# Routing the tiles of the first image between the products of the second image's dynamic convolution

## What is computed

```
x = x + relu(group_norm(conv1x1(concat[xn, dyn_1(xn), dyn_4(xn), dyn_8(xn), dyn_12(xn)])))   # xn = layer norm of x over channels
t = tokens(x)                                        # 2 x 9216 tokens of 256 values
l = layer_norm(t)                                    # over the 256 values
logits = l @ router.T                                # 8 experts
two best experts per token, their softmax weights divided by their sum
t = t + l + sum over the two of weight_e * (gelu(l @ w1[e] + b1[e]) @ w2[e] + b2[e])
```

## Time and profile before

| | us |
|---|---|
| median of three runs | 2617.31 |
| the profiled execution | 2616.45 |
| its span, first to last instruction | 2614.6 |

### The profile page before, as it was taken

How to read it: one execution, slowest core, us unless ns; L and a number is a source line. 1 busy time by engine, 2 the same in 40 slices (tenths; PEclk the granted TensorE clock), 3 DMA queues, 4 the chain that set the end, 5 groups by cost and what they waited for, 6 DMA issues and landing times.

```text
span 2614.6 us, 61081 instructions
## 1 busy us (share of the span) xinstructions
PE 2046.2 (78%) x20292; PEld 1918.8 (73%) x20293; DVE 1624.7 (62%) x4238; ACT 1187.8 (45%) x2441; POOL 1026.5 (39%) x1390
## 2 busy tenths in 40 slices
PE   5887699999688867999994766750799999995332
PEld 4777499999678757999993766650799999994222
DVE  3554475666555545656665867663577899885644
ACT  4654233333256533333333544440577777773211
POOL 4444012233234411223320677777455566563000
PEclk9999599999899977999996655555899999997555
DMA  4332156677433214656766897753566555555887
GB/s 122 91 88 68 47 174 157 158 179 176 123 85 85 79 43 132 170 142 170 174 160 186 277 325 264 257 189 131 164 195 206 172 162 159 150 158 177 289 296 271
DMA packets 328031, 434.91 MB, mean 166 GB/s; under 512 B 86586, under 2 KB 253114, under 8 KB 326778
## 3 DMA queue, kind: packets, MB, share of 16 engines
q1 hardware_dynamic: 273618, 315.07, 42.9%
q0 software_dynamic: 41024, 97.10, 10.7%
q10 hardware_dynamic: 13200, 20.19, 2.1%
HBM read 278.46 MB, written 159.94 MB: 168 GB/s over the span
## 4 chain that ended last, share of the span: by engine, by line
PE 46%; DMA 17%; POOL 15%; issue 10%; DVE 5%; ACT 4%; DVEq 2%; SPq 1%; POOLq 0%; ACTq 0%
PE ps_y L381 16%; POOL expert_in L1786 8%; DMA expert_out<-e_out,dest 7%; PE ps L381 6%; POOL taps L1752 6%; PE ps_o L854 6%; PE ps_a L381 5%; PE ps_b L790 5%; DMA o_y<-expert_out 3%; DMA o_acc<-res_scratch 2%; ACT g_rows L1059 2%; PE ps_f L762 2%; DMA expert_in<-c_ln,pos 2%; PE ps_o L841 1%; PE ps_x L967 1%
## 5 line engine op out<-in xcount | busy, mean ns | idle before, releaser
L381 PE MATMUL ps_y<-cat_hi,wp 128*128 128x288 f32 x2048 | 469.5, 305 | 1.8 <-DVE cat_lo L1370 1.8
L1774 POOL DMA_DIRECT2D patches<-rows_scratch x352 | 194.8, 598 | 651.5 <-PE ps_o L854 492.4
L1809 POOL DMA_INDIRECT expert_out<-e_out,dest x304 | 310.3, 1021 | 237.4 <-DMA expert_out<-e_out,dest 117.4
L1786 POOL DMA_INDIRECT expert_in<-c_ln,pos x288 | 294.4, 1022 | 186.8 <-DVE pos L1515 92.1
L381 PEld LDWEIGHTS ps_y<-cat_hi,wp 128*128 128x128 f32 x2048 | 343.2, 189 | 2.0 <-DVE cat_lo L1370 2.0
L1137 ACT ACTIVATE cat_hi<-ps_o 128x288 fp32r<-128x288 f32 (+1 forms) x576 | 200.1, 386 | 252.9 <-PE ps_o L854 164.2
L381 PE MATMUL ps_y<-cat_lo,wp 128*128 128x288 f32 x1024 | 301.4, 294 | 0.0
L1370 DVE SCALAR_TENSOR_TENSOR cat_lo<-ps_o,cat_hi 128x288 fp32r<-128x288 f32 (+1 forms) x576 | 219.4, 419 | 129.8 <-ACT cat_hi L1137 129.6
L1752 POOL TENSOR_TENSOR taps<-taps,g_rows 96x108 f32<-96x108 f32 (+1 forms) x432 | 200.7, 494 | 242.2 <-ACT g_rows L1059 238.5
L381 PE MATMUL ps<-e_hi,w_now 128*128 128x256 f32 x1216 | 243.8, 284 | 1.2 <-issue 1.1
L381 PE MATMUL ps<-w,h_hi 128*128 x1216 | 234.5, 291 | 5.6 <-DVE h_lo L1658 5.6
(11 more groups left out here) (181 smaller groups left out, 4774.1 us busy)
## 6 DMA issues: line engine op xcount, KB each, us to landing
e_x<-expert_in SPq DMA_DIRECT2D x152, 260.0 KB
o_y<-expert_out SPq DMA_DIRECT2D x48, 768.0 KB, 5.3
patches<-rows_scratch SPq DMA_DIRECT2D x160, 192.0 KB
patches<-rows_scratch SPq DMA_DIRECT2D x256, 108.0 KB
patches<-rows_scratch SPq DMA_DIRECT2D x192, 112.0 KB
x_in<-in_x SPq DMA_DIRECT2D x48, 384.0 KB, 3.3
rows_scratch<-rows_st SPq DMA_DIRECT2D x48, 384.0 KB, 3.1
y_scratch<-y_acc SPq DMA_DIRECT2D x16, 1152.0 KB, 11.6
```

What stands on the lines that cost most here:

```text
L381: mm = eng.matmul(out, lhs[p], rhs[q], start=start and n == 0, stop=stop and n == 2)
L1774: pool.dma_start(patch_target(s, n), patch_source(m, s, n)).then_inc(patch_pooled[s % RING], 16)
L1786: pool.indirect_dma_start(out=xs_dram, out_offset=bass.IndirectOffsetOnAxis(ap=at, axis=0), in_=c_ln[:, v, k // TT, k % TT], in_offset=Non ...
L1809: pool.indirect_dma_start(out=ys_dram, out_offset=bass.IndirectOffsetOnAxis(ap=at, axis=0), in_=e_out[:, u, j], in_offset=None).then_inc(e ...
```

## The change

The first image is routed during the product stage of the second image. A `slot` is a place between two branch products of that stage, one in each step but the first, and two in a step of kind 3, which makes 79. In 72 of them PE turns one tile of 128 tokens and multiplies it by the router (`turn_tile`), ACT and DVE do the statistics, the norm and the residual of that tile, and once for six tiles DVE does `choose` and `place` in pieces of one to four instructions that stand between its other work. The logits are taken from the raw token and corrected by `router_sum` (the sum of the router's rows), so that the second transpose falls away for these tiles. SP loads the blocks and stores a residual per tile, POOL adds x and the convolution's output (`add_block`, one TENSOR_TENSOR of 768 values a partition) and issues the 144 scatters, three in a step. All of this has psum in one bank, `ps_k`, taken from `ps_b`, so `band` now fills one bank in two halves, the second after the step's second tick, in the product stages of both images. The ring of patches falls from 4 to 3. The group norm of the first image is computed at the start of the second image's first stage, six constants are loaded at the program's start, and the routing stage has only the 12 pairs of the second image. EARLY (residual groups kept in SBUF for the combination) falls from 30 to 28 of 48. `w1`, `b1`, `b2` and eight fills are now issued behind the first two pairs' loads of the routing stage; before they were issued halfway through it.

```diff
-RING = 4
+RING = 3
-EARLY = 30
+EARLY = 28
-            ps_b = psum(r1, "ps_b", [128, 2, 512])
+            ps_b = psum(r1, "ps_b", [128, 512])
+            ps_k = psum(r1, "ps_k", [128, 512])
...
+                def turn_tile(t):
+                    j, k = divmod(t, TT)
+                    pe.wait_ge(r_x1, j + 1)
+                    for c in range(CC):
+                        pe.transpose(ps_k[:, c * 128:(c + 1) * 128], r_x[:, j % 2, c, k * 128:(k + 1) * 128], ident[:])
+                    for c in range(CC):
+                        mm = pe.matmul(ps_k[:, 256 + t % TP * E:256 + (t % TP + 1) * E], r_x[:, j % 2, c, k * 128:(k + 1) * 128],
+                                       router[:, c], start=c == 0, stop=c == CC - 1)
+                    mm.then_inc(r_tok, 1)
...
-                        band(s + 1)
+                        band(s + 1, 0)
                     for n in range(CC * parts(s)):
                         branch(s, n // parts(s), n % parts(s))
+                        k = slot_at(m, s, n)
+                        if k is not None:
+                            slot(k)
                         if s and n in (1, 3):
                             project(s - 1, n // 2, 0)
                             project(s - 1, n // 2, 1)
+                        if n == 1 and s + 1 < STEPS:
+                            band(s + 1, 1)
...
+                        t = slot_at(m, s, n, 1)                      # ACT
+                        if t is not None and t < ITILES:
+                            norm_tile(t)
+                            if t % TT == 1 and (t + 2) // TT < ITILES // TT:
+                                relu_block((t + 2) // TT)
...
+                def add_block(j):                                    # POOL
+                    pool.wait_ge(r_relu, j + 1)
+                    flat = lambda z: z.rearrange("p c k -> p (c k)")
+                    pool.tensor_tensor(flat(r_x[:, j % 2]), flat(r_x[:, j % 2]), flat(r_y[:, j % 2]), ALU.add).then_inc(r_x1, 1)
+                def scatter_rows(p, q):
+                    if q == 0:
+                        pool.wait_ge(r_placed, p + 1)
+                    for k in range(3 * q, 3 * q + 3):
...
                 for s in range(STEPS):
+                    while m and blocks < ITILES // TT and slot_step(3 * blocks - 2) + 2 <= s:
+                        add_block(blocks)
+                        blocks += 1
+                    while m and quarters < 4 * CPAIRS and placed_step(quarters // 4) + 3 + quarters % 4 <= s:
+                        scatter_rows(quarters // 4, quarters % 4)
+                        quarters += 1
                     shared = [n for n in range(loads(s)) if second_queue(s, n)]
                     if shared and s >= RING:
                         pool.wait_ge(out_ready, m * UNITS + unit(s - RING + 1))
```

More of the change, by code:

```diff
@@ L443, in build, with slot_at, slot_step, pair_at @@
         UNITS = unit(STEPS)
+        slot_ticks = []
+        for s_ in range(1, STEPS):
+            first = 2 if kind(s_) == 1 and s_ > UNITS1 else 1
+            slot_ticks += [unit(s_) + first] + ([unit(s_) + 5] if kind(s_) == 3 else [])
+        slot_of_tick = {u: k for k, u in enumerate(slot_ticks)}
+        step_of_tick = [s_ for s_ in range(STEPS) for n_ in range(CC * parts(s_))]
+        def slot_at(m, s, n, later=0):
+            k = slot_of_tick.get(unit(s) + n - later)
+            return k if m == 1 else None
+        def slot_step(k):
+            return step_of_tick[slot_ticks[k]]
+        ROUTE_AT, RANK_AT = TP - 1, TP + 2
+        def pair_at(m, s, n, first, later):
+            k = slot_at(m, s, n, later)
+            return (k - first) // TP if k is not None and k >= first and (k - first) % TP == 0 and k < first + ITILES else None
+        def halves(s):
+            return (384, 192) if kind(s) == 3 else (HALF, HALF)
         Y_UNITS = UNITS1 + CLASSES
@@ L534, in _ @@
             sp.dma_start(wg_stage[:], a["w_gen"]).then_inc(consts_in, 16)
+            for dst, src in ((same[:], a["k_same"]), (router[:], a["router"]), (order[:], a["k_order"]),
+                             (before[:], a["k_before"]), (region[:], a["k_region"]), (token[:], a["k_token"])):
+                sp.dma_start(dst, src).then_inc(consts_in, 16)
             leave(sp)
@@ L626, in _ @@
+            with sp.Fori(1, CPAIRS // 2) as t:
+                for v in range(2):
+                    load(t * 2 + v, v)
+                    store(t * 2 + (v - 2))
+            store(CPAIRS - 2)
             sp.wait_ge(cw_lo, 1)
             sp.dma_start(w_stage[:].rearrange("p e c -> p (e c)"), a["w2"]).then_inc(w_loaded, 16)
-            store(PAIRS - 1)
+            store(CPAIRS - 1)
             for u in range(2):
-                wait(sp, c_stored[u], 16 * PAIRS)
+                wait(sp, c_stored[u], 16 * CPAIRS)
@@ new lines, in residual @@
+                def residual(t):
+                    dve.wait_ge(r_lnd, t + 1)
+                    after(dve, r_stored[t % 3], 16 * (t // 3))
+                    dve.tensor_tensor(r_res[:, t % 3], ps_k[:, 0:C], r_ln[:, t // TP % HELD, t % TP, 0:C],
+                                      ALU.add).then_inc(r_resd, 1)
+                every = lambda z: z.unsqueeze(2).broadcast_to([128, TP, E])
+                ranks = order[:].rearrange("p (o e) -> p o e", o=1).broadcast_to([128, TP, E])
+                picked = [0]
```

510 lines of the change are left out of this document (359 added, 151 removed).

## The result

| | before | after |
|---|---|---|
| median of 4 runs, us | 2621.75 (2616.59 to 2630.79) | 2708.89 (2705.59 to 2717.55) |
| ratio | | 1.0334, 95% [1.0292, 1.0375] |
| profiled execution, us | 2616.45, span 2614.6 | 2707.78, span 2705.9 |

The account below looks back on a forecast made before the run. POOL's scatters were taken to bound routing, and PE the second image's product stage. From the profiled execution, 2616.45 - 194 + 95 + 30 + 5 + 3 = 2555 us, with a range of 2480 to 2615 us.

Parts of the forecast that it names:

- Routing, -194: Routing stage: half of the pairs leave, new stage 262 us, a gain of 194 us (ends 165 and 205).
- PE's products, 48 (inside the 95): Second product stage: two transposes and two narrow products more per tile cost PE 48 us, the least growth.
- VectorE's share, 95: Second product stage: the slower of DVE and PE counts in each step; growth 77 us in groups, 18 in strips.
- Late patches, 30: Second product stage: patches late behind POOL's adds and scatters in nine groups, 30 us (ends 0 and 130).
- POOL has the time: 0 for the scatters: Second product stage: POOL's patches, scatters and adds take 53 of 69 us per three groups; no term for scatters themselves.
- First product stage, 5 (0 to 20): First image's product stage: halved bands and three patch buffers cost 5 us, from 0 to 20.
- Transfers in the stage: Second product stage: 19 MB in and 19 out add some 110 us of DMA time, hidden.
- The rest, 3: Combination: two more residual groups cost 2.8 us; constants and group norm 0, at most 5.
- Rival 4: Second product stage: kind 3 patches late by 9 us in every group, growth 252, kernel 2682 us; chance 0.10.
- The rule that I cited from the Trainium skill, SBUF — State Buffer, Who interferes with whom: Two-SBUF-input vector operations and GpSimd operations reading SBUF block each other; 44 us at most, nothing in the sum.
- PE under 85% busy: Sign in the profile after: second product stage 510 to 520 us, DVE busy over 80%, PE under 85%.
- theory 1: Theory after the result, second product stage: ScalarE and VectorE wait for the band's second half, tile moments queued behind.

Follow-up runs that it names:

- x1: The kernel before with one edit, a ring of three patch steps in place of four: 2774.65 us, ratio 1.0160; product stages 405.7 and 408 us.
- e17: e16 with the first image's 144 scatters issued only after the second product stage: that stage 464.3 us, one execution.
- e16: e9 with POOL issuing a step's patches ahead of its additions and scatters: second product stage 583.0 us.
- e9: e4 with the first image's tile moments, deviation, factors, norm and residual also left out: second product stage 615.1 us.
- e4: The changed kernel without the first image's choice of experts, ranking products and counting of places, rows scattered to fixed places: second product stage 670.5 us.
- c0: The changed kernel, no edit, as control on a slower chip: 2811.16 us, ratio 1.0285 to the kernel before; second product stage 702.5 us.
- e10b: The changed kernel with 72 more bn_stats of 256 columns on VectorE, one per tile, results unused: 2823.49 us, ratio 1.0310; second product stage 713.3 us.
- e1: The changed kernel with ScalarE and VectorE taking the next band's second half at the end of tick 1: 2747.86 us, ratio 1.0049; second product stage 644.6 us.
- e18: e16 with the 72 residual stores of 128 KB issued after the second product stage, scatters in place: that stage 573.1 us, one execution.
- e15: The changed kernel with band halves late, patches first, relu and choice under projections, and a ring of four in the first product stage: 2730.15 us, ratio 0.9963.

## Why the prediction was wrong

The second product stage on the slower chips, as a ladder of the runs (each step is a difference of two single profiled stages, each on two chips, in this order of leaving out; another order could share them differently):

| | us | from |
|---|---|---|
| the kernel before with a ring of three | 408 | x1 |
| PE's products, blocks' loads, relu, additions, stores | +56 | e17 |
| scatters beside the products | +119 | e16 - e17 |
| patches behind POOL's other work | +32 | e9 - e16 |
| moments, norms and residuals of tiles, in this order | +55 | e4 - e9 |
| choosing, ranking and placing | +32 | c0 - e4 |
| the changed kernel | 702.5 | c0 |

- **Routing, -194.** Right: -191.8, and 259.9 us for the 262 forecast. Inside it two small errors partly cancel: from first to last scatter it took 195.2 us, not 190, and the head grew by 2, not 5.
- **PE's products, 48 (inside the 95).** Too small: 84 us. I had priced a product by its weight load (0.14); the rows are 255 ns for each of 288 narrow ones and 315 for each of 144 transposes, in a stage with a granted clock of 0.85.
- **VectorE's share, 95. This is the step that failed.** It added the operations of each kind of step and let the busier engine count, PE's 48 included, so 47 were for VectorE beyond PE. DVE's work came in lower than I had it (135 us more, not 179) and DVE is 59% busy, but the ladder's two rows for the tiles' work on VectorE and ScalarE are 55 + 32 = 87 us; and 72 more operations of DVE cost 7 to 11 us, not their 30 (e10b). A good part of the price is where a dependent instruction stands in an in-order engine. My sum had the band in halves as 7 us of DVE work and did not ask what is queued behind `band_lo(s + 1, 1)` while it waits. Moving that block alone, with all work unchanged, gives 58 us (e1). The strips show it on the first chip too, nearly without scatters: 109.5 of their 141.8 us lie before the first one, and they grew by 43.6 us for the 18 of my sum. On the slower chips e1 shortens them from 147.6 to 127.0.
- **Late patches, 30.** The size of the waits was right, 27.8 us in eleven waits (nine of them, 24.9 us, in kind 3 steps, as said). But they overlapped other waits: taking them away gave 10 us. With the tiles' work gone they were worth 32 (e9 to e16).
- **POOL has the time: 0 for the scatters. This term failed too, and on the slower chips it is the largest.** It is true that POOL has the time, and it misled me. I priced scatters in the product stage by POOL's 1.27 us each, and asked only whether it had room. On the slower chips their presence costs 119 us, with instructions of PE, ACT and DVE late. On the first chip the stage was 60 us shorter, all of it after the first scatter, and such waits were nearly absent, so they probably cost less there; how much was not measured. That leaves the 211 us of the groups on that chip without a full account: no experiment ran there.
- **First product stage, 5 (0 to 20).** It was 22.6, outside my ends, and it is the ring (x1), not the band's halves; the second product stage has the same 20 us, for which my sum had nothing. SP's 33.8 us of waits for PE did not show that the fourth buffer was spare: they were waits for that buffer.
- **Transfers in the stage.** I counted 38 MB more. It is 48 (62.9 to 110.9), because the stores' 9.4 MB were left out. By e18 the stores are worth 10 us.
- **The rest, 3.** 6.6 behind the last scatter, and 1 less in the filters' stage.
- Rival 4 had a growth that loses (252 us; it was 254.8), but its mechanism, patches late in all groups, is not what happened.
- The rule that I cited from the Trainium skill, SBUF — State Buffer, Who interferes with whom, was not put to the test. In the trace no operation of VectorE with two SBUF inputs ran at the same time as one of the 24 additions, and the choosing steps took 198 to 207 ns, as in the earlier trace rows.

So theory 1 and the scatters, with the ring, are shown on the slower chips; the scatters' size rests on one execution of e17. Not settled: by what path scatters delay the engines. The trace shows late instructions on PE, DVE and ACT at once, and only 1 MB of instruction transfers in the stage; that these queue behind the scatters' packets would fit, and was not tried. The share of the clock (48 us on PE's old products) is not apart from its causes: the granted clock came back with the waits, to 0.95 in e17 and 0.98 in e15's first stage. Where my forecast of the mechanism held (some 262 us of routing, nine late patches in steps of kind 3, PE under 85% busy), it did not make the growth right: 254.8 us for the 125 forecast.

## What to carry to other kernels

When work is woven into a full pipeline, walk each in-order engine's list and ask at every wait what stands behind it; summing each engine's work per step tells you only the floor. Price moved transfers by what they do to all engines of their new stage, not by their issuing engine's free time, and measure that on more than one chip. That the engine which issues transfers waits for buffers does not show that a buffer is spare: run the smaller depth by itself first.

## What was not expected of the hardware

The same program differs between the first chip and c0's by stage, not evenly: routing took 260 and 299 us, the woven stage 642 and 702, but the filters' stage 303 and 304, the first product stage 405 and 402, and all that follows routing 784 and 792. Only the stages with the indirect scatters differ by more than 2%, and there the engines show waits for instructions: x1's routing, with 288 scatters, took 552 us against the 451.7 of the kernel before on the first chip, with 267 us of such waits on ACT and 137 on DVE (none and 10 on the first chip). The change won more by the shorter routing there (552 to 299 us) and lost as much more in the woven stage, so the two ratios, 1.0334 and 1.0285, hardly differ; their intervals overlap.
